# Both images' attention values joined behind the next row's first turn, with four exponential buffers

## The reference, cut to what matters

```python
x = x + shifted_window_attention(_gn(x), ...)   # 7x7 windows, 8 heads of size 8
x = x + binary_conv(_gn(x), kernel, bias)       # signs, times channel scales and box sums
x = x + ternary_conv(_gn(x), kernel)
x = x + gated_conv_mixer(_gn(x), ...)

# the attention, for each window w and head h (N = 49 tokens)
attn = einsum('whnd,whmd->whnm', q * scale, k) + relative_position_bias + mask
attn = softmax(attn)
out  = einsum('whnm,whmd->whnd', attn, v) @ proj_weight.T + proj_bias

# the scales of the second layer
alpha = mean(abs(kernel), axis=(0, 1, 2))
```

## Time and profile before

| | |
|---|---|
| median of 3 runs | 196.95 us |
| the profiled execution, its own time | 196.93 us |
| its span | 195.1 us |
| PE busy | 182.3 us (93%) |
| DVE busy | 155.4 us (80%) |
| ACT busy | 128.3 us (66%) |
| POOL busy | 107.7 us (55%) |
| TensorE clock granted | 1.00 |

### The profile page before, as it was taken

How to read it: one execution, slowest core, us unless ns; L and a number is a source line. 1 busy time by engine, 2 the same in 40 slices (tenths; PEclk the granted TensorE clock), 3 DMA queues, 4 the chain that set the end, 5 groups by cost and what they waited for, 6 DMA issues and landing times.

```text
span 195.1 us, 6785 instructions
## 1 busy us (share of the span) xinstructions
PE 182.3 (93%) x2751; PEld 130.8 (67%) x2751; DVE 155.4 (80%) x322; ACT 128.3 (66%) x251; POOL 107.7 (55%) x122
## 2 busy tenths in 40 slices
PE   7876989989999999999999999998899999999994
PEld 2445878878898889889987886664456655453330
DVE  3568798978899788987898893799997768957653
ACT  3346778569767997777977757154965339789650
POOL 0339999958432479644595107749644410647560
PEclk9999999999999999999999999999999999999999
DMA  6990000000000000000000000002234521011512
GB/s 190 430 403 12 3 0 5 5 3 2 3 3 3 3 3 3 2 3 3 5 3 3 0 3 3 0 3 47 49 85 112 132 57 41 0 45 30 176 57 107
DMA packets 5021, 9.97 MB, mean 51 GB/s; under 512 B 768, under 2 KB 3840, under 8 KB 4864
## 3 DMA queue, kind: packets, MB, share of 16 engines
q1 hardware_dynamic: 4848, 9.21, 15.1%
q10 hardware_dynamic: 144, 0.34, 0.4%
HBM read 5.03 MB, written 1.61 MB: 34 GB/s over the span
## 4 chain that ended last, share of the span: by engine, by line
PE 74%; DVE 15%; issue 3%; POOL 3%; DMA 2%; ACT 2%; DVEq 0%; ACTq 0%; POOLq 0%
PE turned L833 13%; PE outs L853 12%; PE scores L954 7%; PE scores L820 6%; PE qkv L791 5%; PE turned L1036 4%; PE scores L1010 3%; PE scores L970 3%; PE qkv L803 3%; PE qkv L1024 3%; DVE mx L1196 3%; PE scores L1011 3%; DVE d L1201 3%; PE outs L876 2%; DMA xw<-xw_in 2%
## 5 line engine op out<-in xcount | busy, mean ns | idle before, releaser
L833 PE MATMUL turned<-cst,d 113*113 113x113 f32 x256 | 32.6, 270 | 2.3 <-DVE d L1201 2.0
L214 POOL TENSOR_TENSOR kex<-ks,cst 128x784 f32<-128x784 f32 (+1 forms) x16 | 23.6, 1472 | 19.9 <-ACT ks L519 19.3
L833 PEld LDWEIGHTS turned<-cst,d 113*113 113x113 f32 x256 | 28.6, 178 | 7.8 <-issue 4.7
L510 ACT ACTIVATE scores<-rel 113x784 f32<-113x784 f32 x32 | 26.0, 827 | 10.9 <-DVE d L1201 6.0
L540 ACT ACTIVATE pt<-turned 113x392 f32<-113x392 f32 x64 | 28.3, 493 | 6.3 <-PE turned L833 6.3
L1201 DVE TENSOR_TENSOR d<-scores,mx 113x784 f32<-113x784 f32 x32 | 31.2, 976 | 1.1
L1196 DVE TENSOR_REDUCE mx<-scores 113x16 f32<-113x784 f32 x32 | 30.7, 959 | 1.8 <-PE scores L820 1.7
L853 PE MATMUL outs<-vsb,pt 113*49 113x18 f32 x1024 | 29.2, 199 | 0.2 <-ACT pt L540 0.2
L853 PEld LDWEIGHTS outs<-vsb,pt 113*49 113x49 f32 x1024 | 26.1, 125 | 4.2 <-issue 0.6
L340 POOL TENSOR_TENSOR rstd<-ve,mhalf 128x1 f32<-128x1 f32 (+1 forms) x15 | 8.7, 580 | 24.3 <-DVE ve L1162 24.0
L249 POOL TENSOR_TENSOR kex<-su,sz 128x392 f32<-128x392 f32 x14 | 14.0, 1018 | 12.2 <-ACT su L664 7.1
(11 more groups left out here) (130 smaller groups left out, 376.1 us busy)
## 6 DMA issues: line engine op xcount, KB each, us to landing
p<-parts SPq DMA_DIRECT2D x14, 112.5 KB, 2.2
x<-x_in SPq DMA_DIRECT2D x1, 1568.0 KB, 9.9
out<-xw SPq DMA_DIRECT2D x8, 196.0 KB, 1.9
xs<-xs SPq DMA_DIRECT2D x8, 98.5 KB, 2.1
xw<-xw_in SPq DMA_DIRECT2D x2, 392.0 KB, 4.7
xw<-xw_in SPq DMA_DIRECT2D x1, 784.0 KB, 6.6
ker<-ker_in SPq DMA_DIRECT2D x2, 288.0 KB, 10.3
p3x<-parts SPq DMA_DIRECT2D x8, 60.0 KB, 2.0
```

What stands on the lines that cost most here:

```text
L214: return engine.tensor_tensor(kex[:, par, :, a * WT:b * WT], ks[:, a * WT:b * WT].rearrange("p (o t) -> p o t", o=1).broadcast_to([P, 4, n ...
L510: act.activation(o, i, ACT.Identity).then_inc(seeded, 1)
L833: mm = pe.transpose(ps_t[j][0:WK, n * WQ:n * WQ + WK], d[0:WK, k % 2, h:h + 2, :].rearrange("p a b -> p (a b)")[:, 0:WK], packed)
```

## The change

It does six things.

- `pt` has four buffers in place of two, taken by k modulo 4, and `expo(k)` waits for `values(k - 4)` in place of `values(k - 2)`.
- In rows 2 to 15 PE does `values(2R - 2)` and `values(2R - 1)` together behind `turn(2R)`. Before, `values(2R)` stood between `gather(R - 1)` and `proj_qk(R + 3)`, and `values(2R - 1)` behind `turn(2R)`. The last row keeps its `values(2R)` behind its gather.
- In row 0 PE does `turn(1)` ahead of `scores(1)`, then `proj_v(1)`, both values and `proj_qk(3)`.
- `project(R)` waits for `gn_copied` as `values` does.
- The `alpha` matmul moves from behind `scores(4)` in row 3 to ahead of `scores(5)` in row 4, and the wait for the scales from k = 7 to k = 9.
- On DVE the moments of pair 2 move from row 1 to row 0, `kernel_sums` from row 2 to row 3, and `channel_scales` from the head of row 4 to behind its residual.

```diff
-        pt = sb("pt", [P, 2, 2, NH // 2, WQ])
+        pt = sb("pt", [P, 4, 2, NH // 2, WQ])
...
-                if k >= 2:
-                    act.wait_ge(pv_done, k - 1)
+                if k >= 4:
+                    act.wait_ge(pv_done, k - 3)
...
-                if k == 7 and j == 1:
+                if k == 9 and j == 1:
                     pe.wait_ge(aw_ready, 1)
...
             def project(R):
                 pe.wait_ge(att_ready, R + 1)
                 pe.wait_ge(o_ready, R + 1)
+                pe.wait_ge(gn_copied, copied_by(R + 1))
...
                 turn(2 * R, 1)
                 if R == 0:
                     proj_qk(2)
+                    turn(1, 0)
+                    turn(1, 1)
+                    scores(1)
+                    proj_v(1)
+                    values(0)
+                    values(1)
+                    proj_qk(3)
+                    continue
...
-                if R > 0:
+                if R > 1:
+                    values(2 * R - 2)
                     values(2 * R - 1)
-                if 0 < R < NR - 1:
+                if R < NR - 1:
                     proj_v(R + 1)
+                if R == 4:
+                    pe.wait_ge(asum_ready, 1)
+                    pe.wait_ge(exp_done, 4 * R + 2)
+                    pe.matmul(alpha, cc("ones"), asum[:], start=True, stop=True).then_inc(pe_alpha, 1)
                 if R + 1 < NR:
                     scores(R + 1)
-                if R == 3:
-                    pe.wait_ge(asum_ready, 1)
-                    pe.wait_ge(exp_done, 14)
-                    pe.matmul(alpha, cc("ones"), asum[:], start=True, stop=True).then_inc(pe_alpha, 1)
                 turn(2 * R + 1, 0)
                 turn(2 * R + 1, 1)
-                if R == 0:
-                    proj_v(1)
-                else:
-                    gather(R - 1)
-                values(2 * R)
+                gather(R - 1)
+                if R == NR - 1:
+                    values(2 * R)
                 if R + 3 < NR:
                     proj_qk(R + 3)
-                if R > 0:
-                    project(R - 1)
+                project(R - 1)
```

More of the change, by code:

```diff
@@ L537, in expo @@
                 act.wait_ge(t_done, 2 * k + j + 1)
-                if k >= 2:
-                    act.wait_ge(pv_done, k - 1)
-                act.activation(pt[0:WK, k % 2, j].rearrange("p n (w t) -> p n w t", w=2),
+                if k >= 4:
+                    act.wait_ge(pv_done, k - 3)
+                act.activation(pt[0:WK, k % 4, j].rearrange("p n (w t) -> p n w t", w=2),
                                ps_t[j][0:WK, 0:4 * WQ].rearrange("p (n w t) -> p n w t", n=4, w=2),
@@ L853, in values @@
                                 mm = pe.matmul(ps_o[64 * c:64 * c + WT, 18 * n:18 * n + 18],
-                                               pt[0:WK, k % 2, j, 2 * a + hp, WT * c:WT * c + WT],
+                                               pt[0:WK, k % 4, j, 2 * a + hp, WT * c:WT * c + WT],
                                                vsb[0:WK, R % 2, 2 * (4 * (2 * a + c) + 2 * j + hp) + p, :],
@@ L1266, in _ @@
                 g, r = R // NW, R % NW
-                if R == 4:
-                    channel_scales()
                 shift(2 * R)
@@ L1282, in _ @@
                     variances(1, 1, 2, mixed)
-                if R == 1:
                     dve.wait_ge(ld_x2, 16)
                     window_moments(2)
+                if R == 1:
                     window_moments(3).then_inc(gn_stats, 1)
@@ L1288, in _ @@
                     variances(2, 2, 3, mixed)
+                if R == 3:
                     kernel_sums()
+                if R == 4:
+                    channel_scales()
                 if g > 0 and r == 1:
```

## The result

The changed kernel took 203.65 to 213.49 us in five executions, with a median of 209.28 us over the first four, against 196.94 us before (196.90 to 197.01). The ratio is 1.0371, with a 95% interval of 1.0321 to 1.0421; it leaves out the two executions of 213.4 us, in which the granted clock was 0.944; the one of them with a trace shows it fallen for some 25 us. Because of them the median of 209.28 lies above the forecast range of 203.4 to 208.2. Run again, the changed kernel took 203.78 to 206.51 us, a ratio of 1.0387 (1.0331 to 1.0442). Without a fall of the clock it is 203.8 us (the executions at 1.00 took 203.65 to 203.79): 6.9 us slower. The forecast was 206.1 us.

A forecast was written before the change was run, and what follows sets the result against it. PE was taken to bound most rows, DVE close behind. Rows 0 to 4 +0.4, rows 5 to 12 6.3, row 13 0.85, row 14 0.79, row 15 0.85: 9.2 on 196.93 gives 206.1 us, range 203.4 to 208.2.

The forecast's parts named there:

- the likeliest case: Whole kernel: the forecast itself, slower by 9.2 us at 206.1 us; chance 0.82.
- the copy of `att` is uncovered when the values leave: Between gather and next q and k: PE waits for ACT's copy, a hole of 0.79 us per row.
- The second half of a row: From `turn(2R + 1)` to `turn(2R + 2)`: 3.05 us, where row 8 took 3.11.
- The latency of 0.15: From the end of ACT's copy to the waiting matmul: 0.15 us, with bounds 0 and 0.21.
- The joined values: First half of a row: one more set of values costs 0.85 us, bounded by 0.75 and 0.91.
- DVE as second bound: `weigh` starts 0.85 us later; DVE needs 6.45 us in row 8, hidden under PE's 7.01; row 13 pays 0.85.
- Rows 0 to 4: Early rows: a lead of 1.2 us by `turn(8)`, lost by `turn(10)`; in sum +0.4 us.
- The wait at alpha: Row 4: PE waits 0.5 us for the exponentials of k = 8, and alpha itself takes about 0.3.
- The first, that DVE alone decides: Whole loop: PE does not wait for the `att` copy; ordinary rows 6.45 us, total 200.7 us; chance 0.07.
- The second, rows of 0.3 more: 11 rows: ACT and DVE push into each other, 0.3 us more per row, 209.4 us; chance 0.07.
- the third, slack on PE: Rows 5 to 12: PE is not the bound and absorbs the added values and hole; 195.7 us; chance 0.03.
- The fourth, the clock: Any row: holes drop the clock, up to 6.2 us more for one row, from 212 us; chance 0.01.

The follow-up runs named there:

- the kernel with the gather ahead: Changed kernel with `gather(R - 1)` ahead of `turn(2R + 1)` on PE and the `att` copy ahead of that turn's exponentials on ACT; 202.24 to 207.54 us.
- the kernel with three feeds: Zero matmuls added to the kernel with the gather ahead: 36 in row 13, 18 in row 14, 26 in row 15; 201.10 to 202.05 us.

## Why the prediction was right, and where it was off

The time without a fall, 203.8 us, lies in the range and the likeliest case is the one that happened, but the loss was sized at 9.2 us and is 6.9. That is close to the lower end of the range, 203.4, and by the prediction's own count of its errors it is that end itself (203.8): the range held by the little that was added to it.

- That the copy of `att` is uncovered when the values leave: right, in place, number and size. The second half of a row was put at 1.81 + 0.15 + 1.09 = 3.05; it is 1.80 + 0.15 + 1.07 = 3.02. The latency of 0.15, read from another place in row 0, held to the hundredth.
- The joined values: this is the term that was mis-sized. I took 0.85 us, from the set that stood between gather and q and k. The first half grew by 0.67 only (75.23 - 71.45 = 3.78 against 3.11). The two sets take 1.49 us from start to the next start (72.34 to 73.83), and a single one in that place took 0.76 (70.42 to 71.18 in the trace before), so the second costs 0.73; the step from v to the scores is another 0.07 shorter. I had a set in two places of the trace and took the one that was leaving, not the one that the new set would join. Its 0.76 would have taken away half of the error of 0.18; the rest is the shorter steps behind the pair. The range I gave the term (0.75 to 0.91) did not hold it. Rows 2 to 15 each have such a pair: 14 x 0.18 = 2.5 us, which is about the whole error of 2.3.
- DVE as second bound: right in kind. The weighing starts 74.03 - 71.45 = 2.58 after the turn, 0.74 later than before, for the same reason as above and not 0.85. Row 13 pays 0.73 and is bounded by DVE, row 9 (6.93) is just over the ordinary row.
- Rows 0 to 4: turns 4, 6, 8 and 10 were put at 28.3, 36.0, 43.0 and 50.8 and start at 28.20, 35.68, 42.65 and 50.49. Part of this is luck: in row 2 the first half took 4.13 us (32.33 - 28.20) where I had 4.68, and the second 3.35 (35.68 - 32.33) where I had 3.05, since DVE was late there again by 0.17. The wait at alpha was put at 0.5 and is 0.54:

```profile
43.51 0.97 DVE L1208 TENSOR_TENSOR d<-scores,mx 113x784 f32<-113x784 f32 x1
...
45.28 0.86 ACT L540 ACTIVATE pt<-turned 113x392 f32<-113x392 f32 x2
...
46.29 0.41 PE L920 MATMUL turned<-asum,cst 128*128 128x64 f32 x2 [0.54 <-ACT pt L540]
```

- The rivals. The first, that DVE alone decides (200.7 us), did not happen, but the kernel with the gather ahead is close to it with 201.1. The second, rows of 0.3 more, and the third, slack on PE, did not happen. The fourth, the clock, I gave 0.01, and it did happen in part of the executions: two of the first five were at 213.4 us, outside the range, where I had said that 212 is where it starts. Its place I had wrong. I compared the ordinary row (6.1 busy of 6.8) with a stretch that had kept its clock at 6.95 of 10, and the ordinary rows did keep theirs. But row 13 waits more (5.62 busy of 6.93), and I did not look at the last rows with the clock in mind; and one stretch that kept the clock is no proof that another will. The clock deserved more than the 0.01: with the gather ahead the median was 205.55 us without zeros and 201.25 with three waits filled. The Trainium skill (TensorE: Matmul & The Clock Gate, section Why this matters for your kernels) warns of idle gaps between bursts of matmuls. The runs agree that idle time costs the clock, but the gaps it warns of are longer than any wait here in the attention loop, 1.26 us at most, and the clock fell all the same.

## What to carry to other kernels

Work that stands between a write to a bank and the next write to the same bank covers the copy out of it; before moving such work, look for what the other engine does meanwhile and when it ends (here 1.81 us after the turn, with 1.17 of PE's own work to cover it). Price a moved piece of work by its like at the place where it goes, not at the place that it leaves. Where an order opens small waits on an engine that had none, look at more than one execution: the loss was 6.9 us in most, and another 9.6 came in two of nine.

## What the runs showed of the hardware that I had not expected

- The granted clock fell from 1.00 to 0.50 although no single wait of PE ahead of it was longer than 1.26 us, and in the changed kernel none of the ordinary rows or of row 13 had one longer than 0.71 (row 13 was busy for 5.62 us of 6.93). It stayed down for about 25 us with PE recorded as busy nearly throughout (12.00 of 12.00 us in the stretch shown), and for about 3.5 us in row 3 of the kernel with three feeds.
- With bf16 matmuls of zeros of 28 columns in the waits of the last rows, the clock did not fall there in the profiled execution, and none of six stood below 0.991. They take 0.033 us each (20 in 0.65 us).
- A second set of 16 float32 matmuls right behind its like takes 0.73 us, where a single set took 0.76 ahead of v and 0.85 ahead of q and k.
